# Dispatch with a fixed region of rows per expert, and the last 512 rows normalised after the engines' meeting

## The reference, cut to what matters

```python
x = x + ga * attn(layernorm(x) * (1 + ca) + sa)
h = layernorm(x) * (1 + cb) + sb
routing_probs = softmax(h @ gate_w.T)
topk_w, topk_idx = top_k(routing_probs, 4); topk_w /= topk_w.sum()
shared = silu_mul(h @ shared_gate_up.T) @ shared_down.T * sigmoid(h @ shared_gate_vec.T)
for each expert e:   # 16
    sparse += silu_mul(h @ gate_up[e].T) @ down[e].T * combine[:, e]
x = x + gb * (shared + sparse)
```

## Time and profile before

| | us |
|---|---|
| median of 3 runs (lowest to highest) | 632.84 (631.92 to 635.31) |
| the profiled execution | 636.92 |
| its span, first to last instruction | 635.1 |

### The profile page before, as it was taken

One profiled execution on the slowest core, in us unless ns is written; L12 is line 12 of the kernel. 1 busy time (PEld: TensorE's weight loads), 2 busy tenths in 40 slices (PEclk: granted clock), 3 DMA queues, 4 the chain that ended last, 5 costly groups with the idle time before them and its releaser, 6 DMA issues.

```text
span 635.1 us, 14023 instructions
## 1 busy us (share of the span) xinstructions
PE 541.8 (85%) x4139; PEld 471.7 (74%) x4140; DVE 473.5 (75%) x1197; ACT 283.3 (45%) x696; POOL 321.8 (51%) x390
## 2 busy tenths in 40 slices
PE   4889899999979999994799789977999999999600
PEld 1567677888869889882587568866999999999500
DVE  3588989888743898987675876756777777777478
ACT  3355555556546655441245244425444444444200
POOL 3256776878665474551076757700444444444400
PEclk8889999999999999995789989978999999999855
DMA  9412122224990521112166567686544444442297
GB/s 309 162 57 71 55 73 83 52 74 149 329 311 14 148 76 62 49 58 68 42 186 201 166 212 232 221 252 209 167 133 130 125 132 127 124 131 88 76 382 279
DMA packets 66389, 92.30 MB, mean 145 GB/s; under 512 B 8512, under 2 KB 55360, under 8 KB 66336
## 3 DMA queue, kind: packets, MB, share of 16 engines
q1 hardware_dynamic: 56176, 69.72, 36.2%
q0 software_dynamic: 6864, 18.88, 8.0%
q10 hardware_dynamic: 3296, 3.03, 1.4%
HBM read 53.69 MB, written 35.82 MB: 141 GB/s over the span
## 4 chain that ended last, share of the span: by engine, by line
PE 34%; DVE 8%; issue 4%; DMA 3%; ACT 2%; another core or an unknown queue 1%; SPq 0%; POOL 0%; DVEq 0%; ACTq 0%; POOLq 0%
PE bank L2063 12%; PE bank L1797 5%; PE bank L2081 4%; DVE wda_lo L2028 4%; PE bank L1813 3%; PE bank L2083 3%; PE bank L2047 3%; PE bank L2073 3%; DMA wgu_hi<-results 1%; ACT s_a_hi L1604 1%; DMA stage<-expert_d 1%; DMA stage<-expert_gu 1%; DVE s_a_lo L1720 1%; DMA stage<-shared_d 0%
## 5 line engine op out<-in xcount | busy, mean ns | idle before, releaser
L1931 POOL DMA_INDIRECT results<-yb,xe x79 | 75.8, 959 | 107.1 <-DVE yb L2010 75.6
L1575 POOL DMA_INDIRECT dispatched<-rows,slot x64 | 66.0, 1031 | 40.1 <-issue 17.5
L2063 PE MATMUL bank<-wgu_hi,xT_hi 128*128 x158 | 59.2, 375 | 5.5 <-DVE xT_lo L1991 5.5
L2004 DVE TENSOR_TENSOR e_hT_lo<-bank,e_hT_hi 128x256 fp32r<-128x256 f32 x79 | 33.5, 425 | 32.6 <-issue 20.5
L2063 PE MATMUL bank<-wgu_hi,xT_lo 128*128 x158 | 51.9, 329 | 0.0
L2063 PE MATMUL bank<-wgu_lo,xT_hi 128*128 x158 | 51.9, 329 | 0.0
L736 DVE TENSOR_TENSOR probs<-bank,causal 128x512 f32<-128x512 f32 x64 | 39.8, 684 | 13.6 <-PE bank L926 13.6
L1964 ACT CAST e_hT_hi<-bank 128x256 fp32r<-128x256 f32 x79 | 29.4, 373 | 41.1 <-PE bank L2073 37.9
L1959 ACT ACTIVATE e_sg<-bank 128x176 f32<-128x176 f32 x79 | 25.1, 317 | 50.1 <-PE bank L2063 34.1
L591 POOL TENSOR_TENSOR orms<-omse,neghalf 128x16 f32<-128x16 f32 x16 | 47.1, 2944 | 0.3
L1797 PE MATMUL bank<-h3T_hi,wsg_hi 128*128 128x512 f32 x88 | 38.3, 435 | 6.3 <-DVE hid L1716 2.1
(11 more groups left out here) (234 smaller groups left out, 1854.9 us busy)
## 6 DMA issues: line engine op xcount, KB each, us to landing
dispatched<-fill SPq DMA_DIRECT2D x20, 520.0 KB, 9.0
xe<-dispatched SPq DMA_DIRECT2D x79, 130.0 KB
trig<-t_trig SPq DMA_DIRECT2D x16, 512.0 KB, 3.7
stage<-expert_gu SPq DMA_DIRECT2D x16, 352.0 KB
wgu_hi<-results SPq DMA_DIRECT2D x11, 512.0 KB, 7.7
xt<-L_attn_x SPq DMA_DIRECT2D x32, 128.0 KB, 2.6
wgu_lo<-results SPq DMA_DIRECT2D x5, 512.0 KB, 16.5
x_rows<-h_all SPq DMA_DIRECT2D x16, 128.0 KB, 2.0
```

The lines of the kernel that those rows point to most:

```text
L1575: pool.indirect_dma_start(out=dram["dispatched"], out_offset=bass.IndirectOffsetOnAxis(ap=slot[:, k, t:t + 1], axis=0), in_=rows[:, t, :], ...
L1931: pool.indirect_dma_start(out=dram["results"], out_offset=bass.IndirectOffsetOnAxis(ap=xe[r][:, E:E + 1].bitcast(INT), axis=0), in_=yb[:, ...
L2004: nc.vector.tensor_tensor(hT[1][:, q, :], hT_bank[p][:, 0:2 * P], hT[0][:, q, :].bitcast(F32), ALU.subtract).then_inc(S["h_lo"], 1)
L2063: mm = nc.tensor.matmul(gu_bank[p][:, 0:GU], xT[xn_][:, p, k, :], wgu[wn][:, k, e, :], start=(k == 0 and i == 0), stop=(k == KB - 1 and i ...
```

## The change

1. **Rows of the last group behind the meeting.** The steps of `mlp` for one tile move into a helper, `normalised_rows`, which is called a second time with new semaphores for group 3. Those steps now stand among the first blocks of `shared_and_dispatch`. The stage takes the PSUM banks in another order, so that its first blocks don't use those which still hold group 3. PE waits once (`first`) until DVE has read the early ranks, since the transposes use that bank.
2. **A fixed region per expert.** The dispatch buffer has 2176 rows (REGION) for each expert and 16 empty tiles at the end (EMPTY). A row's slot is its rank plus the expert's region. For the first 10 tiles (EARLY) the slots need nothing of the last 6, so their 40 scatters come first; the other 24 come later. PACE is 4. The fill before is 4 transfers, not 20; in its place SP writes, per expert, one tile of rows and one column of numbers behind the expert's last row (`fill_up`, 32 transfers at addresses read by 16 loads of a value).
3. **Counts in fewer steps.** Counts, bases, the expert and the row of each tile are worked out on 16 partitions and with three small matmul steps; the 16 steps of `experts_of_tiles` go. SP reads each tile's row from `tile_row` before it loads the tile.
4. **Other order.** `low_down` goes from DVE to POOL. The buffers are laid out anew, and no piece is loaded in group 0: the counts are [0]*6, [1]*6, [2,1,2,1,2,1], [2,1,2,1,2,1].

```diff
+REGION = N + P
+EMPTY = NX * REGION
+EARLY = NT - TPG - 2
...
-        for n in range(ETILES // 4):
+        for n in range(NX // 4):
             sp.dma_start(unused[n, :, :, :], fill[:, :, :]).then_inc(s_filled, 16)
...
-        count = [[0, 0, 1, 1, 1, 1], [1] * 6, [1, 2, 1, 2, 1, 1], [1] * 6]
+        count = [[0] * 6, [1] * 6, [2, 1, 2, 1, 2, 1], [2, 1, 2, 1, 2, 1]]
...
+        def fill_up(e):
+            if e == 0:
+                sp.wait_ge(S["free"], 1)
+            row = sp.value_load(first_free[0:1, e:e + 1], min_val=0, max_val=EMPTY)
+            sp.dma_start(dram["dispatched"][bass.ds(row, P), 0:E], gb[:, :]).then_inc(s_filled, 16)
+            with nc.allow_non_contiguous_dma(reason="one index per row"):
+                sp.dma_start(dram["dispatched"][bass.ds(row, P), E:E + 1].bitcast(INT), unfilled[:, e:e + 1]).then_inc(s_filled, 16)
+
         def body(g, q):
             for b in range(NB):
+                if g == 1 and b >= 2:
+                    for e in range((b - 2) * NX // 4, (b - 1) * NX // 4):
+                        fill_up(e)
                 if g and b == 4:
                     for n in range(TPG):
                         store_x4(g - 1, n)
                 for n in pieces(g, b):
                     load_piece(n)
...
+        PACE = 4
...
+        last.inverse_std(LG, 0)
+        last.inverse_std(LG, 1)
         pool.wait_ge(S["tab_in"], 64)
+        number(0, near)
+        number(0, far)
+        low_down(0)
+        last.inverse_std(LG, 2)
+        last.inverse_std(LG, 3)
+        low_down(1)
+        send(0, near, 1, 1)
+        low_down(2)
+        send(0, far, 2, 1)
+        for k in range(1, TOPK):
+            number(k, near)
+            send(k, near, 2 * k + 1, k + 1)
+            number(k, far)
+            send(k, far, 2 * k + 2, k + 1)
...
+        silu(0, 0)
+        high_down(0)
+        last.evacuate(LG, 0)
+        high(0, 0)
+        silu(0, 1)
...
+        def rank_early():
+            dve.wait_ge(S["tab_in"], 64)
+            dve.wait_ge(S["rank_ps"], 1)
+            ranked = b_rank[:, 0:EARLY * NX].rearrange("p (t e) -> p t e", e=NX)
+            nc.vector.tensor_tensor(early_slots[:, :, :], ranked, region.unsqueeze(1).broadcast_to([P, EARLY, NX]), ALU.add).then_inc(S["first"], 1)
+            dve.wait_ge(S["first"], 1)
...
+        def slots(k, late):
+            tiles = slice(EARLY, NT) if late else slice(0, EARLY)
+            chain(nc.vector.scalar_tensor_tensor(pick[:, tiles, :], order[:, tiles, :], float(k), late_slots if late else early_slots[:, :, :],
+                                                 ALU.is_equal, ALU.mult))
+            chain(nc.vector.tensor_reduce(slot32[:, k, tiles], pick[:, tiles, :], AX.X, ALU.add))
+            nc.vector.tensor_copy(slot[:, k, tiles], slot32[:, k, tiles]).then_inc(S["slots"], 1)
...
+        def first_blocks():
+            for i in range(TPG):
+                last.add_residual(LG, i)
+            for i in range(2):
+                last.stats(LG, i)
+                last.centre(LG, i)
+            rank_early()
+            last.modulate(LG, 0)
+            last.keep_logits(LG - 1, TPG - 1)
+            last.compare(LG - 1, 1)
+            product(0, 0)
+            slots(0, False)
+            last.stats(LG, 2)
+            last.centre(LG, 2)
+            last.modulate(LG, 1)
+            low_hidden(0, 0)
+            last.choose(LG - 1, 1)
...
+            last.compare(LG, 0)
+            hidden(0, 2)
+            last.low_part(LG, 2)
+            last.keep_logits(LG, 2)
+            last.choose(LG, 0)
+            slots(2, False)
+            last.low_part(LG, 3)
+            last.keep_logits(LG, 3)
+            last.compare(LG, 1)
+            last.choose(LG, 1)
...
+        first_product(0, 0)
+        early_ranks()
+        pe.wait_ge(S["first"], 1)
+        last.transpose_h3(LG, 0)
+        first_product(0, 1)
+        last.transpose_h3(LG, 1)
+        last.route(LG, 0)
+        second_product(0, 0, 0)
+        first_product(0, 2)
+        last.transpose_h3(LG, 2)
+        last.route(LG, 1)
+        second_product(0, 1, 0)
+        last.transpose_h3(LG, 3)
+        last.route(LG, 2)
+        first_product(0, 3)
+        last.route(LG, 3)
+        second_product(0, 2, 0)
+        first_product(0, 4)
+        count()
+        first_product(0, 5)
+        second_product(0, 3, 0)
+        base_of_experts()
...
     def sync(sp):
         sp.wait_ge(before["g_ps"], SBLOCKS * NG)
+        sp.wait_ge(before["tiles"], 2)
...
-                sp.dma_start(xe[r][:, :], dispatched[j, :, :]).then_inc(s_in[r], 16)
+                row = sp.value_load(tile_row[0:1, bass.ds(j, 1)], min_val=0, max_val=EMPTY + (NX - 1) * P)
+                sp.dma_start(xe[r][:, 0:E + 1], dispatched[bass.ds(row, P), 0:E + 1]).then_inc(s_in[r], 16)
```

More of the change, by code:

```diff
@@ L1078, in mlp @@
     ahead = Ahead()
+    R = normalised_rows(nc, sem, wait, alone, neghalf, ident, modb, h_all, near, early, h3T, rows, logits, order, chosen, before_tile,
+                        ebefore, x3_tiles, outs, b_tr, b_lg, 0, S)
     def chunk(n):
@@ L1435, in shared_and_dispatch, with rows_from @@
-def shared_and_dispatch(nc, io, sb, sem, wait, alone, bank, gb, weights, tile_expert, h3T, rows, logits,
-                        order, chosen, before_tile, ebefore, wsg, wgu, dram, s_filled, s_down, home):
+        R.route(NG - 2, TPG - 1)
+    def rows_from(first):
+        return normalised_rows(nc, sem, wait, alone, neghalf, ident, modb, h_all, near, early, h3T, rows, logits, order, chosen, before_tile,
+                               ebefore, x3_tiles, outs, b_tr, b_lg, first, None)
+    return Stage(sync, gpsimd, scalar, vector, tensor, S, ahead, rows_from)
@@ L1438, in shared_and_dispatch @@
+def shared_and_dispatch(nc, io, sb, sem, wait, alone, bank, gb, weights, tile_expert, tile_row, h3T, rows, logits,
+                        order, chosen, before_tile, ebefore, wsg, wgu, dram, s_filled, s_down, home, last):
     INT = mybir.dt.int32
     NB, LAST = SBLOCKS, SBLOCKS - 1
+    bank = [bank[n] for n in (0, 3, 5, 7, 1, 4, 2, 6)]
+    LG = NG - 1
     RING, SKEW = 3, 2
@@ L1577, in gpsimd @@
+        for i in range(TPG):
+            pool.wait_ge(last.S[f"row_out{i}"], 16)
+        done = 2 * TOPK
+        number(0, near2)
+        number(0, far2)
+        send(0, near2, done + 1, TOPK + 1)
+        send(0, far2, done + 2, TOPK + 1)
+        for k in range(1, TOPK):
+            number(k, near2)
+            send(k, near2, done + 2 * k + 1, TOPK + k + 1)
+            number(k, far2)
+            send(k, far2, done + 2 * k + 2, TOPK + k + 1)
         for t in range(NT):
@@ L1760, in body @@
         def body(g, q):
-            for b in range(NB):
-                if b == SKEW and not (isinstance(g, int) and g == 0):
+            if g == 0:
+                first_blocks()
+            for b in range(3 if g == 0 else 0, NB):
+                if b == SKEW and g > 0:
                     for i in range(TPG):
```

567 lines of the change are left out of this document (310 added, 257 removed).

## The result

The changed kernel takes 638.51 us in the median of 7 runs (635.11 to 641.39), the kernel before 632.84 on the same chip (631.88 to 635.31): a ratio of 1.0081, 95% interval 1.005 to 1.0113. By the ratio it is slower by 5 us; 622 us were forecast. One run of the kernel before and one of the variant `direct`, further down, took over 1300 us, and the ratios leave them out.

The account below looks back on a forecast made before the run. PE bounds the last stage, unchanged; room lay between 285 and 423 us, where PE idled around the meeting and DVE paced group 1. -13.2 - 1.4 + 2.8 + 0.5 + 0.3 = -11.0 from 632.8 gave 622 us, range 617 to 627.

Parts of the forecast that it names:

- Part 2: Group 1: 27.5 us in place of 30.9, 3.4 gained; SP's `fill_up` loses 2.0 of 0 to 4; net 1.4 gained.
- Part 3: Groups 2 and 3, nine pieces each for 8 and 6: late second pieces cost +2.8 us together, ends 0 and 4.7.
- Part 4: Dispatch and last stage: scatters end near 395, SP's value loads delay the down weights; +0.3 us, between -0.4 and +1.2.
- Part 1: Meeting and group 0: first product 16.5 us earlier, group 0 takes 41.5 us; 13.2 gained, ends 18.4 and 8.2.
- Rival (a): Group 0: PE idles in a relay and stays at 1.2 GHz; 48 us or more there, 632 in total; chance 0.18.
- `low_down` on POOL: Three subtractions on POOL, about 6.5 us, slow DVE beside them: 0.5 us lost, of 0 to 2.2.
- Rival (c): Group 1: SP waits for queue room, `fill_up` takes 3.5 us per expert; +26 for +2, 646 us; chance 0.08.
- the three signs that I had named for being wrong: Group 0 over 45 us, SP still in `fill_up` when group 2 starts, or DVE waiting long for PE's transposes.

Follow-up runs that it names:

- direct: Changed kernel with expert_gu pieces loaded straight into their low part's place, six ahead, `fill_up` where it was: 625.2 us, ratio 0.9878 to the kernel before.
- best_rest: best with the load of the rest of the down weights issued right behind the last piece, once the scatters have landed: 624.69 us, ratio 0.989.
- direct_spread: direct with one expert's `fill_up` behind the pieces of each block: 622.85 us, ratio 0.9855 to the kernel before.
- spread_early: fill_spread with 9, 8 and 7 pieces in groups 1, 2 and 3, still through two buffers: 632.38 us, ratio 1.0014 to the kernel before.
- fill_spread: Changed kernel with one expert's `fill_up` behind each block's pieces from group 1 on: 634.77 us, ratio 1.0029 to the kernel before.
- best: direct_spread with the first four tile rows read into registers before the last first product ends: 622.56 us, ratio 0.9848 to the kernel before.

## Why the prediction was wrong

Three steps failed: the loss by SP in group 1 (Part 2), the price of the moved pieces in groups 2 and 3 (Part 3), and, smaller, the start of the last stage (Part 4).

**Part 1, the meeting: right.** Forecast was 16.5 us earlier with an unchanged 1.6 us between. Counted from the start of the routing step that stands last before it in the old order's `mlp` (284.60 in the earlier trace rows, 281.72 above), the first product starts 18.7 us later in the four profiles of the old order and 2.25 us later in the ten of the new one: 16.5 earlier. (The mean starts, 301.75 and 284.7, are 17 apart, since what stands ahead varies.) Group 0 was forecast at 41.5 and took 43.3, DVE in it 34.45 us of work for 32.2: 2 us off. The reason given for its length was wrong in part. I expected the granted clock near 0.8 and it was 0.96, so PE was at its 2.4 GHz level for nearly all of the stretch. In the chain of waits from 283.9 to 327.3, 21 us are DVE's, 12 PE's, 7 ACT's, and from 306 on none is PE's: a hand-over between engines, as I had said, but paced by DVE. Rival (a), the thin cover, did not happen.

**`low_down` on POOL: mis-sized.** I took 0.5 us, of 0 to 2.2, for DVE steps held up beside POOL. Nothing waits long for POOL's subtractions themselves; a 512-wide one took 1.26 to 1.30 us, less than the 2.2 I had drawn from the earlier trace rows. But each of the three held a step of DVE (in time order, POOL then DVE):

```profile
289.24 1.26 POOL L1621 TENSOR_TENSOR wsd_lo<-stage,wsd_hi 128x512 fp32r<-128x512 f32 x1 [0.78 <-ACT wsd_hi L1681]
289.59 1.20 DVE L1418 SCALAR_TENSOR_TENSOR early<-m_xn,m_rstd,modb 128x256 f32<-128x256 f32 x1
...
306.83 1.30 POOL L1621 TENSOR_TENSOR wsd_lo<-stage,wsd_hi 128x512 fp32r<-128x512 f32 x1 [0.35 <-ACT wsd_hi L1681]
306.87 1.54 DVE L1424 TENSOR_TENSOR h3T_lo<-hT,h3T_hi 128x256 fp32r<-128x256 f32 x1
```

The first DVE step takes 0.48 us elsewhere, the second 0.44; beside the subtraction at 298.72 two steps took 2.03 for 0.96. Each time DVE's step ended 0.3 us after POOL's did. That is 2.9 us, where the three `low_down` had cost DVE 2.1 when they were its own, and it is more than the whole of DVE's 34.45 over 32.2. All have both inputs in SBUF, the kind of step for which the prediction expected this; its "near 1 us" was too little. No run put `low_down` back, so what this costs in time is not shown.

**Part 2, group 1: the first step that failed.** Forecast: 27.5 us by DVE and 2.0 lost to SP, 29.5. Measured: 35.1 and 36.3, so 7.6 and 8.8 above DVE's 27.5 for the 2.0. The price of one expert was good, 1.8 us for 1.7, and the end of the last `fill_up` too, 356.6 for 353, though that is 3.6 late. What failed is "I take 2.0 lost of 0 to 4", because I compared only the *last* piece with when it was wanted. Every four experts between two pieces delay the piece behind them, and the next piece can't be issued until SP has come through four more: the pieces left every 7.7 us and more where a block wants one every 4.4. ACT waited 5.15 us for the piece of block 4 and 4.93 for the next. I had seen that the piece of block 2 would wait for its buffer until about 330 (331.67 in the trace), but not that this wait is itself a cost: it stops SP for 8.7 us with twelve experts still to do. With direct loads alone, and `fill_up` in its place, the group took 29.0 us. The DVE part of the step was right: with the fill-ups spread the group took 26.4 us, a gain of 4.5 over before, above the 3.4 I had taken and within its limit of 6.1 (with ten of the 16 `fill_up` in other groups). Rival (c) named the right place but a wrong price: 3.5 us per expert against 1.8. The 3.7 us it was drawn from is SP's issue right behind the 2 MB load of the down weights, at 420.29; in best_rest the issue right behind the same load took 2.84. No issue of a column took more than 0.36. That it waited for room in the queue, as (c) says, is not shown.

**Part 3, pieces in groups 2 and 3: the second step that failed.** Forecast +2.8, at most 4.7. Measured +3.2 and +3.4 in the first profile, +3.5 and +4.3 in the second, so 6.6 to 7.8; in the kernel before with the new counts +3.4 and +4.5. My own sum for group 2, 28.6 us of DVE's work and waits, was nearer to the 29.4 than the 27.7 that I took because "PE's own backlog hides some", for which I had no row. (For group 3 the upper end adds up to 26.6, not 26.4.) I counted a wait of 1.69 for each second piece, taken from a kernel where most such blocks had single ones around them. With the blocks bunched the right measure for group 2 is a rate. A piece of expert_gu holds its buffer from SP's issue to DVE's end: 0.45 + 4.1 (landing) + 0.8 (ACT) + 0.9 (DVE) = 6.2 us, or 3.1 per piece with two buffers. Nine pieces so take 28 us, against PE's 24.8, and group 2 measured 29.4; with direct loads, which lift that limit, 24.1 and 23.3. The old counts had 8 and 6, which take at most 25 and 19. With the 3.6 us that I took for a landing the rate comes to 26 us: I could have worked it out beforehand. Group 3 the rate doesn't explain. Eight of its nine pieces are of expert_d, 0.33 + 3.2 + 0.63 + 0.61 = 4.8 us or 2.4 per piece, about 22 us in all, and it measured 27.5. ACT waits 4.0 us there for five of those pieces, but in all its variants, direct loads or not, the changed kernel's group 3 took 26.3 us or more, and what holds it stays open. An empty group 0 is a stage in which the two buffers carry nothing, and I gave that no price.

**Part 4: the third.** The last scatter ended at 392.5, 2.5 us earlier than forecast. The start of the last stage was wrong by 1.5 to 2 us: from the first `sh` behind the last product to PE's last instruction it took 174.7 us before, 176.5 and 177.1 after, +1.8 and +2.3 for +0.3, above my upper end of 1.2. In the trace SP needs 4.04 us for the first four tiles, 1.76 in the earlier trace rows, and the down weights' load stands behind them:

```profile
416.28 4.04 SPq L2113 DMA_DIRECT2D xe<-dispatched  x4
420.36 0.67 SPq L2115 DMA_DIRECT2D rows<-expert_rest  x1
...
430.21 1.99 ACT L2153 CAST wdt<-rows 128x1024 fp32r<-128x1024 f32 x2 [1.86 <-DMA rows<-expert_rest]
```

But among the kernels that read the values in this place that stretch took 175.0 us (direct_spread), 175.5 (spread_early), 177.2 (direct) and 177.8 (fill_spread), in the four of the old order 174.7 to 175.3; and reading the rows ahead gained nothing that can be told. How much of the 2 us is SP's stays open.

**The sum.** From these measured lengths against those of before: -16.5 + 5.0 + 4.2 + 3.2 + 3.4 + 1.8 = +1.1 for the first profile, and -16.5 + 5.0 + 5.4 + 3.5 + 4.3 + 2.3 = +4.0 for the second (the ratio says +5). Against the -11.0 of the forecast that is 12.1 or 15.0 off: 5.6 or 6.8 in group 1, 3.8 or 5.0 in groups 2 and 3, 1.7 in group 0, 1.5 or 2.0 in the last stage, less the 0.5 kept for `low_down`, which group 0 holds already. None of the three signs that I had named for being wrong came; a sign for pieces that come late in group 1 was missing. With the loads direct and `fill_up` spread the kernel runs at 622.6 to 622.9 us, 9.2 to 9.6 below before on its chip. That is near the forecast, in part by luck: against my terms group 2 is 4.4 us shorter there (23.3 for 27.7) and group 1 3.1, group 0 3.3 longer and group 3 2.9. What is shown is that the gain of the meeting was there and that the way in which the weights were supplied took it and more.

## What to carry to other kernels

When work is moved out of one stage into later ones, check the supply as a rate: the time that one load holds its buffer, from issue to the last reader, over the number of buffers, times the loads in the stage, against the stage's length. Where that comes out longer the buffers set the pace; where it comes out shorter, as in group 3 here, single waits can still cost. A wait per load from a trace where loads were thin is no price for loads that are dense. When instructions are put on a queue that also issues loads, look at the spacing that they give to *each* load behind them, put them behind a load rather than in front, and few at a time, and never behind a wait that they don't need themselves; and where a load's raw data can stand in the place of its own result, staging buffers can go.

## What the runs showed of the hardware

A transfer from SP with an address read at run time costs that queue more than its issue: a value load of 275 to 620 ns, 152 ns of register work, 332 ns for each DMA. In the last stage, where a value load took 268 ns in the median, it made four tile loads 4.04 us in place of 1.76.

A step of DVE with both inputs in SBUF that met one of POOL's 512-wide subtractions, in group 0, ended only 0.3 us after it: 1.20 us for 0.48, 1.54 for 0.44. Later profiles have the same (2.03 for two of 0.48 and 1.53 for 0.44 in best).

The 16 columns of single numbers, written to memory as 4-byte pieces, cost SP 0.33 us each like any other transfer, and no wait in the trace leads to them. The Trainium skill (DMA: Bandwidth & Descriptors, "Specifications") gives transfers below 512 bytes a read-modify-write, which the prediction priced at 1 to 2 us in this stretch; with the fill-ups spread, and six of the 16 columns in it, group 1 ran at a DMA share of 0.70 and took 26.4 us, so no such price is seen. No run took the columns out alone.
